# Two-layer attention kernel: the separate setup stage removed, a product moved, throw-away matmul columns added

## The reference, cut to what matters

```python
# layer 0
xn = layernorm(x)
zn = layernorm_with_scale_and_bias(xn)                 # second norm, ln_scale, ln_bias
q, k, v = split(zn @ w_qkv)                            # 16 heads of 8 features, columns interleaved by 3
att = softmax(q @ k.T / sqrt(8)) @ v                   # full 1024 x 1024 per head
s = xn + att @ w_proj + b_proj
xp = shift_by_one_row(xn)
r = sigmoid((mu_r * xn + (1 - mu_r) * xp) @ W_r.T)
kk = square(relu((mu_k * xn + (1 - mu_k) * xp) @ W_k.T))
x = x + s * silu(r * (kk @ W_v.T))
# layer 1
xn = layernorm(x)
q, k, v = split(xn @ W_attn)
q_l, k_l = mean_of_16_rows(q), mean_of_16_rows(k)      # 64 landmarks
L = softmax(q @ k_l.T); P = iterative_inverse(softmax(q_l @ k_l.T)); N = softmax(q_l @ k.T)
s = (L @ (P @ (N @ v))) @ W_proj
x = x + s * silu(top2_of_8_experts(xn))
```

## Time and profile before

| | |
|---|---|
| time, median of 3 runs | 1463.61 us (1462.28 to 1465.48) |
| time of the profiled execution | 1458.4 us |
| its span | 1456.6 us |
| PE busy | 1285.6 us (88%) |
| DVE busy | 1011.4 us (69%) |
| ACT busy | 863.6 us (59%) |
| POOL busy | 237.3 us (16%) |

### The profile page before, as it was taken

How to read it: one execution, slowest core, us unless ns; L and a number is a source line. 1 busy time by engine, 2 the same in 40 slices (tenths; PEclk the granted TensorE clock), 3 DMA queues, 4 the chain that set the end, 5 groups by cost and what they waited for, 6 DMA issues and landing times. The chain is left out here.

```text
span 1456.6 us, 26151 instructions
## 1 busy us (share of the span) xinstructions
PE 1285.6 (88%) x10385; PEld 612.0 (42%) x10385; DVE 1011.4 (69%) x1313; ACT 863.6 (59%) x1442; POOL 237.3 (16%) x306
## 2 busy tenths in 40 slices
PE   2876999999999999999999878889899699889990
PEld 2651222222222222222222245545799566568870
DVE  3758898988898988898998455554655488522324
ACT  1541888788787787788888844554223266443331
POOL 4110100000000000000000011000643222124460
PEclk9995999999999999999999977875999599989995
DMA  3575033321334422223200031000010111043316
GB/s 80 177 223 111 14 81 78 72 62 43 73 82 108 107 86 43 63 62 63 61 8 11 5 79 44 16 16 0 3 36 29 32 35 43 12 126 95 94 56 179
DMA packets 75205, 94.97 MB, mean 65 GB/s; under 512 B 13236, under 2 KB 44684, under 8 KB 74052
## 3 DMA queue, kind: packets, MB, share of 16 engines
q1 hardware_dynamic: 69996, 83.19, 22.6%
q0 software_dynamic: 5088, 10.12, 2.2%
HBM read 54.30 MB, written 38.56 MB: 64 GB/s over the span
## 5 line engine op out<-in xcount | busy, mean ns | idle before, releaser
L586 DVE TENSOR_REDUCE b_mx<-psum 128x2 f32<-128x1024 f32 x512 | 601.2, 1218 | 69.4 <-PE psum L667 68.3
L644 ACT ACTIVATE b_exp_ring<-psum 128x512 f32<-128x512 f32 x1024 | 555.5, 599 | 157.2 <-PE psum L703 153.9
L703 PE MATMUL psum<-b_q,b_k 75*128 75x512 bf16 x1024 | 311.3, 386 | 6.7 <-DMA b_q<-b_neg 5.1
L679 PE MATMUL psum<-b_exp_ring,b_v 128*32 128x512 f32 x2048 | 273.5, 606 | 0.9 <-ACT b_exp_ring L644 0.7
L703 PEld LDWEIGHTS psum<-b_q,b_k 75*128 75x128 bf16 x1024 | 79.2, 97 | 321.9 <-ACT b_exp_ring L644 222.8
L665 PE MATMUL psum<-b_k,b_q 64*128 64x512 bf16 x512 | 169.2, 395 | 26.3 <-DVE b_mx L586 13.1
L667 PE MATMUL psum<-b_ko,b_qo 64*128 64x512 bf16 x512 | 169.2, 395 | 0.0
L718 POOL CAST b_neg<-b_neg_rest 16x128 bf16<-16x128 f32 x32 | 9.0, 281 | 660.3 <-DVE b_neg_rest L597 660.3
L665 PEld LDWEIGHTS psum<-b_k,b_q 64*128 64x128 bf16 x512 | 44.4, 93 | 129.3 <-DVE b_mx L586 46.7
L1783 ACT ACTIVATE e_hT<-psum,e_b 128x358 f32<-128x358 f32 (+3 forms) x96 | 53.5, 560 | 74.0 <-PE psum L1803 70.6
L679 PEld LDWEIGHTS psum<-b_exp_ring,b_v 128*32 128x32 f32 x2048 | 41.2, 108 | 108.2 <-issue 106.4
(11 more groups left out here) (275 smaller groups left out, 1503.1 us busy)
## 6 DMA issues: line engine op xcount, KB each, us to landing
b_q<-q_ops SPq DMA_DIRECT2D x48, 192.0 KB
b_k<-k_ops SPq DMA_DIRECT2D x48, 192.0 KB
k_ops<-a_k SPq DMA_DIRECT2D x20, 256.0 KB, 3.2
x_disp<-b_zeros SPq DMA_DIRECT2D x13, 320.0 KB
e_x<-x_disp SPq DMA_DIRECT2D x8, 520.0 KB
v_ops<-a_vs SPq DMA_DIRECT2D x4, 1024.0 KB, 5.5
b_v<-v_ops SPq DMA_DIRECT2D x16, 256.0 KB
av_out<-b_acc SPq DMA_DIRECT2D x128, 32.0 KB, 1.7
```

What stands on the lines that cost most here:

```text
L586: nc.vector.reduce_max(mx[:, d % 2, :, i // 2, i % 2], pair, AX.X).then_inc(sem("b_max_done"), 1)
L644: act.activation(ex[:, n % E_RING, :], g.bank(5 + n % 3), ACT.Exp, scale=ATT_SCALE)\
L679: last = nc.tensor.matmul(AV[32 * i:32 * i + 32, :], v[s][:, at_v:at_v + 32], ex[:, (4 * group + i) % E_RING, :], start=(kb == 0), stop=(k ...
L703: nc.tensor.matmul(g.bank(5 + n % 3), k[s][0:XROWS, h, kb * P:(kb + 1) * P], q[s][0:XROWS, h, half * BANK:(half + 1) * BANK], start=True, ...
```

## The change

- The setup block is gone. Its work stands in `layer0_inputs`: SP loads batch 0 of x first, with a semaphore of its own for each batch, then the ten small loads with w_qkv last, then batches 1 to 3, then four loads that are needed later. The raw weights lie in the tiles `a_pr` and `a_sg`, which are free until batch 0 is nearly done. DVE waits for the weights after the statistics of batch 0, and scales them between xn(0) and zn(0); stats(1) comes after zn(0). PE's transposes of the weights use banks 4 and 5, and PE waits for the scaled weights before the first product.
- PE makes kk before r; ACT takes sigmoid of r behind the second parts of q and k.
- The first five items of maxima (`FIRST = 5`) are done at the end of `layer0_inputs`: item 0 behind r of the last batch, items 1 to 4 behind kv. DVE reduces item 0 behind its third parts, and items 1 to 4 between L363 and the gate. The attention block runs 20 items ahead in place of 25.
- In `layer0_outputs`, `busy(768)` issues two matmuls (512 and 256 columns, float32) before `transposed(c, 0)` of couples 1 to 3, three times a batch, twelve in all. Their result in D0 is overwritten. The wait for the copied-out transposes now stands ahead of the one for the exponentials.

```diff
--- before.py
+++ after.py
-def setup(g, ctx):
-    ...
-            for b in range(B):
-                sp.dma_start(g.X[:, b * TB:(b + 1) * TB, :], xin[:, b * TB:(b + 1) * TB, :])\
-                  .then_inc(sem("setup_moved"), 16)
-    ...
@@ layer0_inputs @@
+    g.mx = keep("b_mx", [P, 2, 2, TB, 2])
...
+    raw, wrkv = pr[:, 0:3 * D], sg[:, 0:3 * D].rearrange("p (i d) -> p i d", i=3)
+    wg, b1raw = sg[0:E, 3 * D:4 * D], sg[0:E * HC, 4 * D:5 * D]
...
@@ layer0_inputs, vector @@
             def stats(b):
+                dve.wait_ge(sem(f"a_x{b}"), 16)
...
+            def first_maximum(n):
+                dve.wait_ge(sem("b_max_scores"), n + 1)
+                pair = g.bank(2 * (n % 2), 2).rearrange("p (h x) -> p h x", h=2)
+                nc.vector.reduce_max(g.mx[:, 0, :, n // 2, n % 2], pair, AX.X).then_inc(sem("b_max_done"), 1)
...
             stats(0)
+            dve.wait_ge(sem("w_loaded"), 16 * 10)
+
+            for c in range(3):
+                nc.vector.tensor_copy(g.wqkv0[:, c, :], raw.rearrange("p (n c) -> p n c", c=3)[:, :, c])
+            link(nc.vector.tensor_scalar(g.cols[:, 4:6], g.cols[:, 2:4], -1.0, 1.0, ALU.mult, ALU.add))
+            g.dve_steps = link.n
+            xn(0)
+            dve.wait_ge(sem("wT_ready"), 1)
+            for i, pair in enumerate((g.wr2, g.wk2)):
+                for n, w in enumerate(pair):
+                    nc.vector.tensor_scalar(w[:, :], g.bank(4)[:, i * P:(i + 1) * P],
+                                            g.cols[:, 2 + 2 * n + i:3 + 2 * n + i], None, ALU.mult)
...
+            nc.vector.tensor_copy(g.b1T[:, :], g.bank(5)[:, 0:E * HC]).then_inc(sem("w_ready"), 1)
+            zn(0)
             stats(1)
-            xn(0)
-            zn(0)
...
                 third(b, 1)
+                if b == B - 1:
+                    first_maximum(0)
...
+                if b == B - 1:
+                    for n in range(1, FIRST):
+                        first_maximum(n)
                 dve.wait_ge(sem("a_sigp"), b + 1)
...
@@ layer0_inputs, scalar @@
             keep_xnT(0)
+            act.wait_ge(sem("w_loaded"), 16 * 10)
             keep_znT(0)
...
-                act.wait_ge(sem("a_r"), b + 1)
-                if b >= 1:
-                    act.wait_ge(sem("a_prod"), b)
-                act.activation(rg[:, :], D1, ACT.Sigmoid).then_inc(sem("a_sigr"), 1)
                 act.wait_ge(sem("a_kk"), b + 1)
...
                     act.activation(part[j][1][:, :], res[j][:, :], ACT.Copy).then_inc(sem("a_part2"), 1)
+                act.wait_ge(sem("a_r"), b + 1)
+                if b >= 1:
+                    act.wait_ge(sem("a_prod"), b)
+                act.activation(rg[:, :], D1, ACT.Sigmoid).then_inc(sem("a_sigr"), 1)
...
@@ layer0_inputs, tensor @@
+            def first_maxima(lo, hi):
+
+                for n in range(lo, hi):
+                    if n >= 2:
+                        pe.wait_ge(sem("b_max_done"), n - 1)
+                    maxima_scores(g, g.q0[0], g.k0[0], g.qo[0], g.ko[0], n, 0, n).then_inc(sem("b_max_scores"), 1)
...
             transposed_x(0)
             transposed_z(0)
+            pe.wait_ge(sem("w_ready"), 1)
...
                 last.then_inc(sem("a_kk"), 1)
+                for t in range(TB):
+                    dst = D1[:, t * P:(t + 1) * P]
+                    nc.tensor.matmul(dst, now[:, t * P:(t + 1) * P], g.wr2[0][:, :], start=True, stop=False)
+                    last = nc.tensor.matmul(dst, before[:, t * P:(t + 1) * P], g.wr2[1][:, :], start=False, stop=True)
+                last.then_inc(sem("a_r"), 1)
                 if b + 1 < B:
                     transposed_x(b + 1)
+                else:
+                    pe.wait_ge(sem("b_loaded0"), LOADS0)
+                    pe.wait_ge(sem("a_vs"), B)
+                    first_maxima(0, 1)
                 pe.wait_ge(sem("a_kact"), b + 1)
                 pe.wait_ge(sem("a_res"), 2 * b + 2)
                 rows_times(nc, D3, kaT, g.wvT[:, :]).then_inc(sem("a_kv"), 1)
                 if b + 1 < B:
                     transposed_z(b + 1)
+                else:
+                    pe.wait_ge(sem("a_sigr"), B)
+                    first_maxima(1, FIRST)
...
+FIRST = 5
+
+
+def maxima_scores(g, q, k, qo, ko, n, p, i):
+
+    t, keys = slice(i // 2 * P, i // 2 * P + P), slice(i % 2 * BANK, i % 2 * BANK + BANK)
+    g.nc.tensor.matmul(g.bank(2 * (n % 2)), q[0:MROWS, 2 * p, t], k[0:MROWS, 2 * p, keys], start=True, stop=True)
+    return g.nc.tensor.matmul(g.bank(2 * (n % 2) + 1), qo[MROWS:P, p, t], ko[MROWS:P, p, keys], start=True, stop=True)
...
@@ layer0_attention, vector and tensor @@
-            for n in range(upto(0, -1)):
+            for n in range(FIRST, upto(0, -1)):
                 item(n)
...
@@ layer0_outputs, tensor @@
+                def busy(columns):
+
+                    lo = 0
+                    while lo < columns:
+                        n = min(BANK, columns - lo)
+                        nc.tensor.matmul(D0[:, 0:n], g.wqkv1[:, 0:P], xT[:, 0:n], start=True, stop=True)
+                        lo += n
+
                 def transposed(c, s):
                     k = PAIRS * b + 2 * c + s
-                    pe.wait_ge(sem("c_en"), k + 1)
                     if c:
                         pe.wait_ge(sem("c_enT"), k - 1)
-                    else:
+                        if s == 0:
+                            busy(3 * BANK // 2)
+                    pe.wait_ge(sem("c_en"), k + 1)
+                    if c == 0:
                         pe.wait_ge(sem("c_v"), 2 * (b + 1))
...
@@ two_layers @@
         g = make(nc, ctx, ins)
-        setup(g, ctx)
         layer0_inputs(g)
```

More of the change, by code:

```diff
@@ L467, in _ @@
                 rows_times(nc, D0, znT, g.wqkv0[:, 2, :]).then_inc(sem("a_v"), 1)
-                for t in range(TB):
-                    dst = D1[:, t * P:(t + 1) * P]
-                    nc.tensor.matmul(dst, now[:, t * P:(t + 1) * P], g.wr2[0][:, :], start=True, stop=False)
-                    last = nc.tensor.matmul(dst, before[:, t * P:(t + 1) * P], g.wr2[1][:, :], start=False, stop=True)
-                last.then_inc(sem("a_r"), 1)
                 pe.wait_ge(sem("a_res"), 2 * b + 1)
```

121 lines of the change are left out of this document (47 added, 74 removed).

## The result

| | before | after |
|---|---|---|
| median | 1462.94 us, 4 runs (1460.98 to 1465.48) | 1420.51 us, 4 runs (1419.00 to 1422.80) |
| ratio, 95% interval | | 0.971 [0.969, 0.9731] |
| profiled execution, span | 1458.4, 1456.6 us | 1420.72, 1419.0 us |
| measured again on another chip (e9) | 1461.67 us, 9 runs | 1424.28 us, 5 runs; 0.9736 [0.9715, 0.9756] |

The change saves 42.4 us, or 37.4 us by the second measurement. The forecast was 1431, with a range from 1422: right in direction, 10.5 us too high, and its range missed the first measurement by 1.5 us.

What follows compares the result with a forecast made beforehand. The prediction took the kernel as a chain of blocks in which whatever one block saves is passed on whole. Its terms summed to -32.6 us, from 1458.4 to 1425.8, or 1431 beside the median 1463.6; range 1422 to 1447.

Steps and rivals of the forecast that it cites:

- the last step of the sum: From 1425.8 us to 1431, because the old kernel's profiled execution lay 5.2 us below the median of its runs.
- First product: Start of the kernel: without the setup block, the first product comes at 18.9 us in place of 31.07, -12.2 us.
- Slow first products: Batch 0 of the inputs: the first products may run at half speed, +1.5 us, bounds 0 and 3.7.
- Period: Batches of the inputs: kk first removes PE's idle 1.50 us ahead of kv, three periods, -4.5 us.
- End of the inputs: Last batch up to the attention block: 22.1 us with the five items in place of 21.0, +1.1 us.
- start of the attention block: Five items fewer, but maxima's stores wait behind loads: scores 24.4 us after the block's start, not 27.4; -3.0 us.
- the bound that I set for an empty queue: Start of the attention block: -5.7 us if the queue held nothing back, first score 21.7 us after the block.
- Filler: layer0_outputs: throw-away columns fill PE's idle 1.59 us and hold the clock, -15.5 us, bounds -20.1 and +24.
- The filler buys nothing: Rival, layer0_outputs: the clock falls for another reason or at each batch's first uncovered gap; 1446 us, chance 0.15.
- The early part gives half: Rival, inputs: late weights, slow PE in batch 0 or a late store lose 7 us of 17; 1438 us, chance 0.13.
- The slower rival: Rival, layer0_outputs: fillers at the lower level add 2.0 us to couples of 8.30; 1488 us, chance 0.04.
- The filler runs at half speed: The slower rival's claim, layer0_outputs: PE's being busy doesn't bring the clock back, batches of 41.3 us; 1488 us, chance 0.04.

Runs made afterwards that it cites:

- e9: The changed kernel measured once more with no edit, on another chip: 1424.28 us, ratio 0.9736 to the kernel before.
- e1: The kernel before, run once more with no edit and with its own trace: 1462.02 us, ratio 1.0002.
- e2: The kernel before with only the throw-away columns of layer0_outputs added: 1443.23 us, ratio 0.9866 to the kernel before.
- e10: The changed kernel with throw-away products from the start, in the gaps between PE's first transposes: 1422.07 us, ratio 0.9723 to the kernel before.
- e5: The changed kernel with r before kk again on PE and sigmoid before relu on ACT: 1445.87 us, ratio 0.98 to the kernel before.
- e7: The changed kernel with the stores of the first maxima issued between the loads of slot 1 and slot 2: 1435.53 us, ratio 0.9747 to the kernel before.
- e6: The changed kernel with no item of maxima moved, all 25 in the attention block: 1437.76 us, ratio 0.9754 to the kernel before.
- e3: The changed kernel without the throw-away columns in layer0_outputs: 1443.09 us, ratio 0.9885 to the kernel before.
- e8: The changed kernel with 1280 more throw-away columns ahead of the first couple of batch 3 of layer0_outputs: 1431.72 us, ratio 0.972 to the kernel before.
- e12: The changed kernel with the filler's products using 32 rows of the operands in place of 128, same columns: 1439.01 us, ratio 0.9839 to the kernel before.
- e11: The edits of e10, e7 and e8 together on the changed kernel: 1417.87 us, ratio 0.9695 to the kernel before.

## Why the prediction was wrong, point by point

**The bottom line.** 10.5 us too high. Two steps failed: the tail of a batch in the filler's term, taken at 8.74 us where it measured 7.85, and the last step of the sum, which added 5.2 us. A smaller miss, 0.95, lies in the first product. In the trace's own terms the sum was -32.6 and the measured difference -37.6: 5.0 us. The other 5.4 us come from the last step, "that execution lay 5.2 below the median of the runs, so beside the median 1463.6 it is 1431", and from the 0.2 by which the new kernel's profiled execution lay above its own median. That step carried the offset of one execution of the old kernel over to the new one. e1 shows what the offset held: the first products at the full level (1.5 us), a faster attention stage (2.3) and rest (1.8). None of it says how the new kernel's executions lie about their median. Part of the miss is chance: e9 has the changed kernel at 1424.3 us, 3.8 above the first measurement, and by it the forecast was 6.7 too high and within its range.

**First product (-12.2, measured -13.15).** The landings were right to 0.1 us. The 0.95 us are xn at 9.33 in place of 9.8, and 8.59 us from there to the product in place of 9.1. The 4.87 us taken from the statistics to xn had the statistics of batch 1 in them, which now come later; xn now waits for POOL's reciprocal root instead (the bracket at 9.33).

**Slow first products (+1.5).** The size was right in this trace (batch 0 took 1.53 more than the steady 17.32), and against the one trace of before, which had none of it, the charge was right. Against the kernel before as it usually runs it was too high: two of its three traces (e1 and the one with the filler, e2) have slow first products as well. Above their steady period the first batches took 0, 1.44 and 1.97 us in the three traces of kernels with the old start, and 1.47 to 2.95 in the nine traces with the new one that have no warm-up. That they are a matter of the clock is shown by e10.

**Period (-4.5).** 17.32 us in place of the 17.6 forecast; e5 confirms the mechanism with 19.09.

**End of the inputs (+1.1) and start of the attention block (-3.0).** 22.15 against 22.1 and 24.44 against 24.4. The mechanism was right in both, and e7 gives the bound that I set for an empty queue. The 24.2 us for the landing of the maxima fits the end of the loads and a microsecond more, which is what the trace shows; the 8.4 us of the store of q, set beside it, would have made 16.3 + 8.4 = 24.7, and these much smaller stores took 7.0. What I did not see is that the sum of the two says that the items were better left in place: e6 splits +1.1 into -2.65 for the order and +3.83 for the items, and 3.83 is more than the 2.78 that they save.

**Filler (-15.5, measured -20.1).** The largest term, and the one mis-sized. The mechanism was right (e2, e3). I had taken the tail of a batch at 8.74 us, worked out from a batch in which it was partly slow; at the full level it takes 25.04 - 3 x 5.73 = 7.85. That is 0.9 each in batches 1 and 2; batch 0 took 25.67, 0.2 under the forecast, and batch 3 29.34 in place of 30.5. These make 3.1; with 1.4 for the way to the first transposes (14.96 us after, 16.38 before), which differed between 14.95 and 16.45 in the other traces without such a cause, it is the 4.6 up to rounding. The forecast kept the tail slow on no other ground than that the trace showed it so. In this trace the full level held through all four tails. It doesn't always: of the nine traces with a filler of 128 rows five have one slow tail each. So part of this gain is luck. The seven of them without e8's filler had stages of 158.5 to 162.1 us, 160.2 on average, and the four traces without a filler 177.8 to 181.1, 179.1 on average; by these the filler gives 18.9 us, 3.4 more than the forecast, and 1.2 of the 4.6 are chance.

**The rivals.** "The filler buys nothing" fell: e3 against the change. The Trainium skill ("TensorE: Matmul & The Clock Gate", "Why this matters for your kernels") warns in that section only of idle gaps a good deal longer than the 1.59 us of the earlier trace rows; the measurement decides, and filling gaps of that size brought 17.7 us in e2. "The early part gives half" did not occur. The slower rival did not occur with 128 rows and occurred in one batch with 32. "The filler runs at half speed" was thus a real danger: in batch 3 of the changed kernel the first filler did (2.77 us), and what e12 changed, the rows of the products, decided whether the level came back behind it.

What stays open: why the clock falls in one batch in one execution and in another in the next, and why the runs of the kernel before spread over 12 us (1457.28 to 1469.04) in 12 runs of e1 while those with the filler spread over 3 (1441.29 to 1444.31, 4 runs of e2). That the filler removes places where the clock can fall would explain it, but that is only argued: the differences between the two traces of the kernel before lie mostly in other stages, and e5, which has the filler, spread over 8.5 us in 4 runs. The same idle 1.59 us did not always bring the fall: in batch 1 of e1 it came at the third such gap, and in batches 0 and 2 of the kernel before about a microsecond behind the gap, within the scores. Other sizes of the filler were not tried.

## What to carry to other kernels

Where identical instructions show two durations a factor of two apart in one trace, look at the granted clock and at the idle time ahead of the first slow one, and try to fill that gap with products over all 128 rows that fit into it; what it can gain is the whole slow stretch behind the gap, not the gap. When work is moved ahead to shorten a wait, price it in its new place and look at the queue in which its result travels: here five items cost more where they went than they saved, until three small stores were put ahead of thirteen large loads. And never carry the offset between one profiled execution and the median over to the changed kernel: profile the old kernel twice, or give the median of the new one its own uncertainty.

## What the runs showed of the hardware that I had not expected

- Products of 32 rows keep PE busy for about the same time (1.55 us at the full level, 1.46 with 128 rows), but did not bring the clock back as those of 128 did: 122.3 us for the four batches against 105.1 and 106.5, and a batch of 41.68 us at 0.52 with PE busy for 41.63 of them (e12), where the level came back around the first filler in the seven traces with 128 rows and the same 2.55 us gap.
- A store of 4 KB behind 26 loads on SP's queue took 7.0 us to land. It took 1.7 us in e7, where the 13 loads ahead of it were through, and 1.8 in the kernel before, where the loads ended about a microsecond after its issue.
- The clock column and the durations disagree at PE's first work. In the window of the first products of the changed kernel (17.90 to 23.10) the column reads 1.00, yet the eight products took 5.24 us where they take 3.70 later. With PE kept busy from the start they took 3.60 (e10), so there the durations tell the level and the column does not.
- With all couples filled, the clock still fell now and then in a tail, behind idle times of 0.95 and 0.5 to 1.1 us close together: in one batch each of e2, e5, e9, e10 and e11, and in none of the changed kernel's first trace, e6, e7 and e8. Each costs 1.7 to 2.7 us against the same batch of the changed kernel's first trace.
